# Attention row sums: VectorE adds 256 columns of two steps in one operation, GpSimd 768 of each step

## What is computed

```python
sim = jnp.einsum('bhid,bhjd->bhij', q, k)
attn = jax.nn.softmax(sim, axis=-1)
out = jnp.einsum('bhij,bhjd->bhid', attn, v)
out = jnp.transpose(out, (0, 2, 1, 3)).reshape(b, m, INNER)
return out @ Wo
```

## Time and profile before

| | |
|---|---|
| median of 3 runs | 2217.95 us (2217.94 to 2218.29) |
| the profiled execution's own time | 2220.97 us |
| its span | 2219.2 us |
| mean granted TensorE clock | 0.987 |
| TensorE, VectorE, ScalarE, GpSimd busy | 2130.5, 1602.3, 1102.6, 918.0 us |

### The profile page before, as it was taken

One profiled execution on the slowest core, in us unless ns is written; L12 is line 12 of the kernel. 1 busy time (PEld: TensorE's weight loads), 2 busy tenths in 40 slices (PEclk: granted clock), 3 DMA queues, 4 the chain that ended last, 5 costly groups with the idle time before them and its releaser, 6 DMA issues. The chain is left out here.

```text
span 2219.2 us, 37466 instructions
## 1 busy us (share of the span) xinstructions
PE 2130.5 (96%) x12720; PEld 1078.2 (49%) x12819; DVE 1602.3 (72%) x2346; ACT 1102.6 (50%) x1732; POOL 918.0 (41%) x643
## 2 busy tenths in 40 slices
PE   6899999989999999999899999999999999999977
PEld 3444444423333333333475665757566475755633
DVE  7677777659989899987565756667575666757673
ACT  4123323334444444555564655656465565647545
POOL 3335555459999999600222203122130222204045
PEclk9999999989999999999999999999999999999988
DMA  3445544433223322432323332342333334233413
GB/s 125 142 162 178 193 163 167 161 96 96 86 86 93 92 86 88 123 112 66 126 96 114 99 122 86 133 124 77 115 104 115 105 126 131 77 114 86 137 40 114
DMA packets 159854, 252.73 MB, mean 114 GB/s; under 512 B 11507, under 2 KB 63987, under 8 KB 159731
## 3 DMA queue, kind: packets, MB, share of 16 engines
q1 hardware_dynamic: 159730, 250.96, 35.3%
HBM read 211.73 MB, written 36.70 MB: 112 GB/s over the span
## 5 line engine op out<-in xcount | busy, mean ns | idle before, releaser
L67 PE MATMUL scores<-xt_hi,wt_hi 128*128 128x256 f16 (+3 forms) x1568 | 413.1, 275 | 10.9 <-DVE xt_lo L1503 5.2
L69 PE MATMUL scores<-xt_hi,wt_lo 128*128 128x256 f16 (+3 forms) x1568 | 412.9, 275 | 0.4
L68 PE MATMUL scores<-xt_lo,wt_hi 128*128 128x256 bf16 (+3 forms) x1560 | 410.3, 275 | 0.0
L1460 POOL TENSOR_TENSOR l_rstd<-l_var_eps,neg_half 128x1 f32<-128x1 f32 x71 | 67.0, 944 | 827.0 <-DVE l_var_eps L1514 827.0
L986 DVE TENSOR_REDUCE pmax<-mx 128x1024 f32 (+1 forms) x196 | 240.1, 1225 | 43.2 <-PE mx L1170 29.3
L69 PE MATMUL l_tok<-wt_hi,h_lo 128*128 128x512 f16 x576 | 218.4, 379 | 1.7
L1743 ACT ACTIVATE wt_hi<-stage 128x512 f16<-128x512 f32 x384 | 213.6, 615 | 8.8 <-DMA stage<-in_L_attn_Wf 8.8
L1183 PE MATMUL scores<-q_hi,res 128*128 128x512 f16 x544 | 209.4, 385 | 2.2 <-DMA res<-keys 2.1
L1184 PE MATMUL scores<-q_lo,res 65*128 65x512 f16 x544 | 208.3, 383 | 0.0
L67 PE MATMUL l_tok<-wt_hi,h_hi 128*128 128x512 f16 x512 | 194.1, 379 | 0.0
L68 PE MATMUL l_tok<-wt_lo,h_hi 128*128 128x512 bf16 x480 | 182.0, 379 | 0.0
(11 more groups left out here) (348 smaller groups left out, 4725.9 us busy)
## 6 DMA issues: line engine op xcount, KB each, us to landing
stage<-in_L_attn_Wf SPq DMA_DIRECT2D x60, 1024.0 KB, 5.3
keys<-wt_hi SPq DMA_DIRECT2D x136, 128.0 KB
res<-keys SPq DMA_DIRECT2D x68, 256.0 KB, 3.3
vb<-values SPq DMA_DIRECT2D x68, 256.0 KB, 5.6
stage<-in_ctx SPq DMA_DIRECT2D x16, 1024.0 KB, 10.1
values<-wt_lo SPq DMA_DIRECT2D x16, 1024.0 KB
stage<-in_L_ffn_f SPq DMA_DIRECT2D x16, 1024.0 KB, 5.3
res<-keys SPq DMA_DIRECT2D x68, 128.0 KB, 5.3
```

Of the source, the lines that this page charges most:

```text
L67: pe.matmul(out, lh, rh, start=first, stop=False, **kw)
L68: pe.matmul(out, lh, rl, start=False, stop=False, **kw)
L69: return pe.matmul(out, ll, rh, start=False, stop=last, **kw)
L1460: g.tensor_tensor(rstd[:, t:t + 1], var_eps[:, t:t + 1], k.neg_half[:, 0:1], ALU.pow).then_inc(rstd_done, 1)
```

## The change

The exponential buffers become the four parts of one tile `xf`, one behind the other, so that an operand can take the same columns of two of them. VectorE's share in the first three pairs becomes 256 columns (`MINE`). It adds them after every second step only: the last 256 columns of both steps, 512 elements a partition, to an accumulator of its own, `twin`, that holds the sum of the even steps beside that of the odd ones. `dve_summed` then rises by two. GpSimd adds columns 0 to 767. `sums` keeps its 1024 columns, of which the last 256 stay zero in these pairs. The row sums take two matmuls of 256 columns more, one for each half of `twin`, into the place of the last 256 columns. ScalarE clears the twin of the next pair as it clears `sums`, GpSimd the first one, and `sums_cleared` counts both. The last pair is as before.

```diff
--- before.py
+++ after.py
@@ -838,7 +838,8 @@
     nc = k.nc
     STEPS = KB * SUB
     P_BUFS = 4
-    CUT = [2 * TOK - P] * (PAIRS - 1) + [0]
+    MINE = 2 * P
+    CUT = 2 * TOK - MINE
     FIRST_PIECE = KB - PIECES
     TURN = KB - 2
 
@@ -854,7 +855,9 @@
 
         ka, kh, k_loaded, km = k.ka, k.kh, k.k_loaded, k.km
         vb = [sb(f"vb{n}", [P, SUB, P], F32) for n in range(2)]
-        probs = [w[:].rearrange("p c n -> p (c n)").bitcast(F32) for w in (k.xt_hi, k.xt_lo, k.f_hi, k.f_lo)]
+        all_probs = k.xf[:].bitcast(F32)
+        probs = [all_probs[:, n] for n in range(P_BUFS)]
+        twin = [sb(f"twin{n}", [P, 2, MINE], F32) for n in range(2)]
         sums = [rows(k.h_lo, 8, 4), slots(k.wt_lo, 0, 1, F32, 2 * TOK)[:, 0]]
         rmax = sb("rmax", [P, UNITS], F32)
         rneg = sb("rneg", [P, UNITS], F16)
@@ -958,10 +961,11 @@
                 pool.sem_inc(pool_summed, P_BUFS)
                 g.memset(zero[:], 0.0).then_inc(consts, 1)
                 g.memset(sums[0], 0.0).then_inc(sums_cleared, 1)
+                g.memset(twin[0][:], 0.0).then_inc(sums_cleared, 1)
                 for p in range(PAIRS - 1):
-                    mine = slice(0, CUT[p])
+                    mine = slice(0, CUT)
                     total = sums[p % 2]
-                    pool.wait_ge(sums_cleared, p + 1)
+                    pool.wait_ge(sums_cleared, 2 * p + 2)
                     with pool.Fori(0, KB) as b:
                         for j in range(SUB):
                             step = p * STEPS + SUB * b + j
@@ -995,12 +999,17 @@
 
                 def row_sum(p, b, j):
                     step = p * STEPS + SUB * b + j
-                    mine = slice(CUT[p], 2 * TOK)
-                    total = sums[p % 2]
-                    dve.wait_ge(exp_done, 2 + step + 1)
-                    dve.wait_ge(dve_summed, P_BUFS + step)
-                    v.tensor_tensor(total[:, mine], total[:, mine], probs[j][:, mine], ALU.add)\
-                        .then_inc(dve_summed, 1)
+                    if p == PAIRS - 1:
+                        total = sums[p % 2]
+                        dve.wait_ge(exp_done, 2 + step + 1)
+                        dve.wait_ge(dve_summed, P_BUFS + step)
+                        v.tensor_tensor(total, total, probs[j], ALU.add).then_inc(dve_summed, 1)
+                    elif j % 2:
+                        total = twin[p % 2]
+                        dve.wait_ge(exp_done, 2 + step + 1)
+                        dve.wait_ge(dve_summed, P_BUFS + step - 1)
+                        v.tensor_tensor(total[:], total[:], all_probs[:, j - 1:j + 1, CUT:2 * TOK], ALU.add)\
+                            .then_inc(dve_summed, 2)
 
                 def weight_low(p, b):
 
@@ -1036,7 +1045,7 @@
                 dve.sem_inc(dve_summed, P_BUFS)
                 pair_max(0)
                 for p in range(PAIRS):
-                    dve.wait_ge(sums_cleared, p + 1)
+                    dve.wait_ge(sums_cleared, 2 * p + 2 - p // 3)
                     if p == PAIRS - 1:
                         for b in range(KB):
                             if b == FIRST_PIECE + 1:
@@ -1114,6 +1123,10 @@
                     a.activation(sums[p % 2].rearrange("p (a n) -> p a n", n=P),
                                  k.ones[:].unsqueeze(1).to_broadcast([P, 2 * TOK // P, P]), ACT.Copy, scale=0.0)\
                         .then_inc(sums_cleared, 1)
+                    if p < PAIRS - 1:
+                        a.activation(twin[p % 2][:].rearrange("p t (a n) -> p (t a) n", n=P),
+                                     k.ones[:].unsqueeze(1).to_broadcast([P, 2 * MINE // P, P]), ACT.Copy, scale=0.0)\
+                            .then_inc(sums_cleared, 1)
 
                 negate_maxima(0)
                 row_maxima(0)
@@ -1215,8 +1228,12 @@
                     pe.wait_ge(pool_summed, P_BUFS + (p + 1) * STEPS)
                     pe.wait_ge(rows_done, 2 * min(p + 2, PAIRS))
                     for s in range(2):
+                        shared = s == 1 and p < PAIRS - 1
                         m = t_.matmul(side[s * HD:(s + 1) * HD, :], k.ones[:, 0:HD],
-                                      sums[p % 2][:, s * TOK:(s + 1) * TOK], start=True, stop=True)
+                                      sums[p % 2][:, s * TOK:(s + 1) * TOK], start=True, stop=not shared)
+                        for n in range(2 if shared else 0):
+                            m = t_.matmul(side[s * HD:(s + 1) * HD, TOK - MINE:TOK], k.ones[:, 0:HD],
+                                          twin[p % 2][:, n, :], start=False, stop=n == 1)
                     m.then_inc(sums_ready, 1)
 
                 def block_steps(p, b, i=0):
@@ -2418,8 +2435,9 @@
         k.wt_hi = sb("wt_hi", [P, CHUNKS, 4, D], F16)
         k.wt_lo = sb("wt_lo", [P, CHUNKS, 4, D], BF16)
         k.stage = sb("stage", [P, STAGES, 4, D], F32)
-        k.xt_hi, k.f_hi = (sb(n, [P, CH, TOK], F16) for n in ("xt_hi", "f_hi"))
-        k.xt_lo, k.f_lo = (sb(n, [P, CH, TOK], BF16) for n in ("xt_lo", "f_lo"))
+        k.xf = sb("xf", [P, 4, CH * TOK], F16)
+        k.xt_hi, k.xt_lo, k.f_hi, k.f_lo = (
+            k.xf[:, n].bitcast(BF16 if n % 2 else F16).rearrange("p (c n) -> p c n", c=CH) for n in range(4))
         k.cst = sb("cst", [P, C_COLS], F32)
         k.ctl = sb("ctl", [P, CH, EX], F32)
         k.bias_rows = sb("bias_rows", [EP, P], F32)
```

## The result

The changed kernel takes **2247.99 us** (median of 4 runs, 2247.49 to 2249.82) against 2217.94 us for the one before (median of 4 runs, 2216.34 to 2218.29): a ratio of 1.0139, 95% interval 1.0123 to 1.0155. It is slower by 30 us. The granted clock is 0.988 (before 0.987).

The account below looks back on a forecast made before the run. TensorE's own work was taken as the bound. Losses +29.4, row sums +2.7 and removed stalls -1.0 sum to +31 us: 2252 on the profiled 2220.97, less 3.0 to the median, so 2249 us; range 2222 to 2267.

Parts of the forecast that it names:

- TensorE's own work is the whole period: In the first three head pairs, TensorE's work fills the 4.36 us of two steps: 3.72 plus 0.64 for maxima matmuls.
- GpSimd's operation at 1.81 us: GpSimd's addition of 768 columns in place of 896 was to take 1.81 us, 1.79 to 1.83 by the rows.
- The prediction's other reading: GpSimd timed start to start: 1.84 against 1.88 us, back 0.08 us sooner per period; first rival holds, +47 for +31.
- The held add ends 0.54 behind GpSimd: A VectorE add standing behind a GpSimd operation was to end 0.54 us after that operation's end.
- the operation behind an add 1.67 behind the add: A GpSimd operation of 768 columns pushed back by VectorE's add was to end 1.67 us after the add's end.
- GpSimd now comes 0.06 us earlier each period, until it starts just ahead of the add: GpSimd's next operation at 8.17 against VectorE's request at 8.23; gaining each period, it causes one loss in six steps.
- the rival of a loss every second period: GpSimd 0.04 quicker or winning against a 0.06 lead: third add lost too, 51 x 0.89 = 45.4, 2265 us; chance 0.28.
- 33 losses at 0.89, +29.4: Over 102 two-step periods, one held add in three delays TensorE's odd maxima matmul by 0.89 us: +29.4 us.
- Row sums +2.7: The two added matmuls of 256 columns on TensorE's path cost 0.9 us, three times: +2.7 us.
- What it can remove is the stall at each of two turns: At two turns between head pairs, a stall of about 0.5 us each goes away: -1.0 us in all.
- The third rival: No steady loss: GpSimd's round reaches 4.36 us or more, the add always comes first; 2220 us, up to 2225; chance 0.22.
- VectorE was the bound: Rival: VectorE sets the pace, its work falls to 3.14 from 4.36, kernel gets faster by some us; chance 0.03.

Follow-up runs that it names:

- e3: The changed kernel with VectorE's share at 288 columns in place of 256 and GpSimd's at 736: 2258.17 us, ratio 1.0182.
- e6: The changed kernel with VectorE's share at 240 columns in place of 256 and GpSimd's at 784: 2224.46 us, ratio 1.0032.
- e4: The kernel before with 256 columns for VectorE and 768 for GpSimd, added after each step, no twin or pairing: 2217.61 us, ratio 0.9997.
- e8: The changed kernel with VectorE's add replaced by a one-input reduction of the same 512 elements, leaving out part of the row sums: 2220.38 us, one run.
- e1: The changed kernel plus an idle GpSimd memset of 128 columns after each odd step's add: 2241.05 us, ratio 1.0104.
- e7: The changed kernel's pairing with the old split, VectorE 2 x 128 columns in one operation, GpSimd 896: 2221.26 us, ratio 1.0015.
- e5: The changed kernel plus an idle GpSimd memset of 256 columns, double that of e1: 2222.41 us, ratio 1.0017.

## Why the prediction was right

The forecast was 2249.0 us for 2247.99, inside 2222 to 2267, with 0.87 on slower. Its mechanism was the one measured; that it came within 1 us owes something to errors that cancel. By its steps:

- **TensorE's own work is the whole period: right.** Every undisturbed interval is still 2.17 or 2.19, in the change and in all eight experiments, and in an undisturbed period of the change VectorE is idle 0.96 us before a reduce (547.38).
- **GpSimd's operation at 1.81 us: right**, 1.806 median. The gap of 0.07 measured 0.078 to 0.080. The prediction's other reading timed GpSimd from start to start, as the Trainium skill says in Perfetto Trace Analysis, "GPSIMD Engine Instruction"; it drew a line from 1.23 at 512 columns, got 1.84 at 768 and a loss in every second period, +47. Measured start to start two operations of 768 columns are 1.88 us apart, as the sum had it: at its own size the page's way of timing and the sum agree, and the line was off. That rival, which had 0.28, is out as the steady pattern; e3 shows it 32 columns further.
- **The held add ends 0.54 behind GpSimd, the operation behind an add 1.67 behind the add: right**, 0.548 and 1.68.
- **"GpSimd now comes 0.06 us earlier each period, until it starts just ahead of the add": the step was half wrong.** Whenever the add goes first, GpSimd's operation starts anew from the add's end, so nothing adds up over rounds. Each round by itself is 4.32 to 4.33, 0.03 to 0.045 short of 4.36, and that is enough: the fourth add meets GpSimd 0.03 to 0.045 ahead. The order it led to, one loss in six steps, stands in most of the trace. The margin on which the rival of a loss every second period hung, the third add's lead, was put at 0.06 and measured 0.10 to 0.12. In six places the next loss came after four steps all the same, behind an interval of 2.33 or 2.37 that the forecast doesn't have: TensorE starts its scores 0.48 to 0.52 us after the maxima matmul and not 0.32 (as at 542.33), the third add is asked for 0.16 later, and its lead is gone. What delays the scores there the profile doesn't show.
- **33 losses at 0.89, +29.4: too high.** There are 28 at 0.83, 23.1, with the six short ones 24.1. Each is 0.06 shorter, since GpSimd is already 0.03 to 0.045 into its operation when the add is asked for, and the reduce behind a held add takes 1.21 and not 1.23. Of the missing five some fell to the turns, where the rhythm starts anew each time.
- **Row sums +2.7: right**, 0.86 three times, 2.6.
- **"What it can remove is the stall at each of two turns", -1.0: wrong.** The old stall is gone, but held adds bring three others; a turn costs 0.9 more without its row sums, +1.8 in all. The start of the attention gave back 1.0, which the sum didn't have; its cause isn't shown.
- **The sum.** +31 was forecast on the profiled execution and +26.5 measured there; on the medians it is +30. The profiled executions can't carry more than some 3 us of precision, and the forecast is no better than that.
- **The third rival decides "at 0.03 us of the operation": right.** With 16 columns more for GpSimd, an operation 0.033 longer, the losses are gone but for one at each turn (e6). The rule of the Trainium skill, SBUF — State Buffer, "SBUF: two separate sides", that who starts first has the pair for the whole instruction, held for every margin above 17 ns. Both engines' held operations end 0.13 us sooner after the other's end than they would take alone (0.548 for 0.681, 1.68 for 1.804), so the wait is a whole operation but for that. Below 17 ns the recorded starts and the rule disagree, and the record of e6 is what counts. That VectorE was the bound had 0.03 and is refuted by e4 and e8.

## What to carry to other kernels

When two engines exclude each other and both run in step with a third, their busy shares tell nothing of the cost: work out who arrives first in each round, to some 10 ns, with the measured length of every part of the round. The time is then a step in the split, not a slope: 240 columns cost 2224 us, 256 columns 2248. Between such neighbours a little *more* work on the engine that arrives too early can be the cure, and a form of the operation with one input from SBUF removes the meeting altogether (e8, which leaves a sum out).

## What was not expected of the hardware

- GpSimd needs a recorded start at least 17 ns ahead to be first: with 12 ns or less (e6, 76 meetings) the add always won, with 20 or more (the change, 28) never, and at 17 both were seen (e1, e3).
- Whether a kernel placed on that edge spreads more isn't shown: e1's four runs lie 6.8 us apart and the four of the change 2.3, but the ten of e7, which has no close meeting, 5.8.
- A memset of 0.20 us between two additions of GpSimd delays the second by 0.01 to 0.04 only (e1), and one of 0.31 us by 0.13 (e5): most of the first is hidden.
